# A message-passing network kernel: the first stage's front and second sorting pass are re-ordered, and its scatters may run three block steps further ahead

## The reference

```python
h = jnp.maximum(_layernorm(x, axis=-1), 0.0)
# resmlp(x) = silu(x + silu(silu(x) @ w1 + b1) @ w2 + b2) @ wout
xx = resmlp0(h)
xs, xp, xd = resmlp1(h)[src_j], resmlp2(h)[src_j], resmlp3(h)[src_j]
s = xx + segment_sum(gs * xs, idx_i)
p = segment_sum(gp * xp[:, None, :], idx_i);  d = segment_sum(gd * xd[:, None, :], idx_i)
pa, pb = split(p @ w_pp);  da, db = split(d @ w_pd)
y = s + (pa * pb).sum(-2) + (da * db).sum(-2)
x = x + resmlp4(y)
```

## Time and profile before

| what | us |
|---|---|
| median of 3 runs | 1198.83 (1195.27 to 1198.98) |
| the profiled execution, its own time | 1192.66 |
| its span, from first to last instruction | 1189.2 |
| what lies around the span | 3.46 |
| TensorE busy | 1093.1 (92% of the span), granted clock 0.971 in the mean |
| VectorE, ScalarE, GpSimd busy | 689.1, 738.0, 465.2 |
| first stage: span's start to TensorE's last product of it | about 414 |
| second stage: TensorE's first transposition | 426.83 |

### The profile page before, as it was taken

How to read it: one execution, slowest core, us unless ns; L and a number is a source line. 1 busy time by engine, 2 the same in 40 slices (tenths; PEclk the granted TensorE clock), 3 DMA queues, 4 the chain that set the end, 5 groups by cost and what they waited for, 6 DMA issues and landing times.

```text
span 1189.2 us, 22906 instructions
## 1 busy us (share of the span) xinstructions
PE 1093.1 (92%) x6267; PEld 713.8 (60%) x6267; DVE 689.1 (58%) x2415; ACT 738.0 (62%) x1379; POOL 465.2 (39%) x429
## 2 busy tenths in 40 slices
PE   4878998968999849999999999999979999999998
PEld 2655665745666425666666666666736666666665
DVE  8876876774666316575666556565633444444432
ACT  4657778856777815656655655566536666666664
POOL 2355666034566542665566556555440000000000
PEclk9989999997999959999999999999998999999999
DMA  8667677745664452665655555555549999999984
GB/s 262 201 222 239 216 229 226 286 140 171 199 224 167 162 93 62 120 119 105 103 107 102 104 99 104 101 102 96 103 68 233 277 274 276 271 274 269 269 276 142
DMA packets 319188, 210.81 MB, mean 177 GB/s; under 512 B 204085, under 2 KB 240831, under 8 KB 318964
## 3 DMA queue, kind: packets, MB, share of 16 engines
q1 hardware_dynamic: 280770, 164.67, 50.1%
q0 software_dynamic: 24208, 19.29, 10.2%
q10 hardware_dynamic: 14112, 25.70, 6.1%
HBM read 107.15 MB, written 102.42 MB: 176 GB/s over the span
## 4 chain that ended last, share of the span: by engine, by line
PE 81%; issue 6%; DVE 5%; SPq 2%; ACT 2%; DMA 2%; another core or an unknown queue 1%; POOL 0%; ACTq 0%; POOLq 0%; DVEq 0%
PE quad L1122 7%; PE bank L1136 7%; PE bank L1758 6%; PE quad L871 5%; PE quad L1128 5%; PE bank L1768 5%; PE bank L888 5%; PE bank L1834 4%; PE quad L878 4%; PE bank L1804 4%; PE bank L1835 4%; PE quad L856 2%; PE quad L1111 2%; PE bank L1807 2%; PE quad L1843 2%
## 5 line engine op out<-in xcount | busy, mean ns | idle before, releaser
L1410 POOL DMA_INDIRECT node_sums<-rowout,row_i x98 | 155.4, 1585 | 49.5 <-issue 29.0
L74 POOL DMA_INDIRECT yin<-node_h,er x98 | 99.3, 1014 | 156.6 <-DMA nxt<-edges_by_src 125.0
L1043 DVE TENSOR_TENSOR rowout<-bank,xin 128x512 f32<-128x512 f32 x98 | 67.8, 691 | 142.7 <-PE bank L1136 141.7
L486 POOL DMA_INDIRECT edges_by_src<-pay,rank_i x98 | 97.1, 990 | 103.8 <-DVE rank_i L689 51.3
L888 PEld LDWEIGHTS bank<-wo_sb,s 128*128 128x128 f32 x720 | 95.8, 196 | 60.5 <-issue 60.5
L1136 PEld LDWEIGHTS bank<-wo_sb,s 128*128 128x128 f32 x784 | 102.8, 191 | 47.8 <-issue 47.8
L1462 DVE SCALAR_TENSOR_TENSOR h<-bank,b_sb,hT 128x512 f32<-128x512 f32 (+1 forms) x75 | 55.4, 739 | 125.4 <-PE bank L1768 122.9
L486 POOL DMA_INDIRECT edges_by_low<-pay,rank_i x98 | 97.5, 995 | 68.8 <-issue 27.6
L781 ACT ACTIVATE xn<-xin,nbias,rnorm 128x128 f32<-128x128 f32 x222 | 106.5, 493 | 15.3 <-DVE nbias L604 10.9
L677 DVE SCALAR_TENSOR_TENSOR picked<-bank,onehot 128x256 bf16<-128x256 f32 (+1 forms) x196 | 67.6, 388 | 80.5 <-PE bank L844 59.3
L888 PE MATMUL bank<-wo_sb,s 128*128 128x128 f32 x720 | 98.3, 280 | 10.6 <-issue 7.3
(11 more groups left out here) (210 smaller groups left out, 2279.3 us busy)
## 6 DMA issues: line engine op xcount, KB each, us to landing
xin<-in_x_dram SPq DMA_DIRECT2D x196, 256.0 KB
node_h<-xn SPq DMA_DIRECT2D x98, 256.0 KB
out_dram<-rowout ACTq DMA_DIRECT2D x98, 256.0 KB
node_sums<-rowout SPq DMA_DIRECT2D x90, 256.0 KB
yin<-node_sums SPq DMA_DIRECT2D x53, 256.0 KB, 3.7
yin<-node_sums SPq DMA_DIRECT2D x180, 64.0 KB, 3.2
src_in_every_row<-edge_src_row SPq DMA_DIRECT2D x24, 256.0 KB
border_sums_by_tile<-border_sums SPq DMA_DIRECT2D x24, 256.0 KB, 2.1
```

The lines of the kernel that those rows point to most:

```text
L74: pool.indirect_dma_start(out=xg[:, s, j, :], out_offset=None, in_=x, in_offset=bass.IndirectOffsetOnAxis(ap=er[:, s, j, 1:2].bitcast(mybi ...
L486: nc.gpsimd.indirect_dma_start(out=ps.dram, out_offset=bass.IndirectOffsetOnAxis(ap=rank_i[:, t:t + 1], axis=0), in_=pay[:, t, :], in_offs ...
L1410: nc.gpsimd.indirect_dma_start(out=ysum, out_offset=bass.IndirectOffsetOnAxis(ap=row_i[:, t % 2, j:j + 1], axis=0), in_=urow[:, t % 2, j, ...
```

## The change

1. **Front.** The first batch of statistics that is made into scales is now of two blocks, not four, and the second of six (blocks 2 to 7). The statistics of blocks 2 and 3, and the comparison of digits (`same_digits`), are put between the first batch's norm steps. SyncE issues the stores of h of blocks 0 to 3 between the loads of x of blocks 9 to 19, where all twelve loads stood ahead of them. One group of counts goes from (3, 1) to (4, 0), the seeds stand where they stood, written as a place.
2. **Turn (second pass).** TensorE's counts begin at (49, 1) and end at (52, 1) rather than (53, 0), in groups of growing number. Seeds and bases are at (53, 0) and (53, 1), the picks of chunk 0 at VectorE's step 52 rather than 54, and `chunks` is 53 rather than 54, so that every later chunk comes one step earlier. The comparison of digits is made before the wait for the counts, and the corrections are made by GpSimd, ahead of its scatters. The norm steps of the batch of blocks 56 to 63 (four in each of VectorE's steps 50 to 54 before) stand in steps 53 and 54, ten in each.
3. **Scatters.** `keep_pace` counts from three block steps earlier in both passes: 2 to 42 in the first, 50 to 90 in the second.

```diff
--- before.py
+++ after.py
...
@@ -281,13 +281,13 @@
             m = 0
             BANK_X = (psum[0], psum[1], psum[2], psum[6])
             BANK_A, BANK_COUNT, BANK_RUN, BANK_O = psum[3], psum[4], psum[5], psum[7]
-            places = ((1, 0), (1, 1), (2, 0), (2, 1), (2, 1), (3, 0), (3, 1), (3, 1), (3, 1), (4, 0), (4, 0), (4, 0), (4, 0), (4, 0))
-            again = tuple(p for p in ((50, 0), (50, 1), (51, 0), (51, 1), (52, 0), (52, 1), (53, 0)) for _ in range(2))
-            passes = (Pass(0, {0: (0, 14)}, places, 4, 3, 5, (0, 5), by_low, LOW),
-                      Pass(1, {49: (0, 14)}, again, 53, 54, 54, (49, 54), by_src, HIGH))
+            places = ((1, 0), (1, 1), (2, 0), (2, 1), (2, 1), (3, 0), (3, 1), (3, 1), (4, 0), (4, 0), (4, 0), (4, 0), (4, 0), (4, 0))
+            again = ((49, 1), (50, 0), (50, 1)) + ((51, 0),) * 2 + ((51, 1),) * 2 + ((52, 0),) * 3 + ((52, 1),) * 4
+            passes = (Pass(0, {0: (0, 14)}, places, (4, 1), (5, 0), 3, 5, (0, 5), by_low, LOW),
+                      Pass(1, {49: (0, 14)}, again, (53, 0), (53, 1), 52, 53, (49, 54), by_src, HIGH))
             LN_OPS = 20
             LARGE = 32
-            batches = [(b, 4) for b in range(0, LARGE, 4)] + [(b, min(8, NB - b)) for b in range(LARGE, NB, 8)]
+            batches = [(0, 2), (2, 6)] + [(b, 4) for b in range(8, LARGE, 4)] + [(b, min(8, NB - b)) for b in range(LARGE, NB, 8)]
 
             x_in = [sem(f"n_x_in{i}") for i in range(NX)]
             stored = [sem(f"n_stored{i}") for i in range(4)]
@@ -333,6 +333,8 @@
                         todo = {3: range(1, CH + 1), 4: range(CH + 1, LN_OPS + 1)}
                     else:
                         first, steps = (b - 5, 4) if b <= LARGE else (b - 6, 5)
+                        if any(ps.n and first <= ps.picked_at < first + steps for ps in passes):
+                            first, steps = passes[1].picked_at + 1, 2
                         each = -(-LN_OPS // steps)
                         todo = {first + n: range(1 + each * n, 1 + min(each * (n + 1), LN_OPS)) for n in range(steps)}
                     if B and k in todo:
@@ -429,10 +431,10 @@
                 assert n_rest == N_REST
                 for b in range(8, NX):
                     load_x(b)
-                store_h(0)
-                store_h(1)
+                    if b % 3 == 0:
+                        store_h(b // 3 - 3)
                 for k in range(2, NB + 4):
-                    if k < NB:
+                    if 4 <= k < NB:
                         store_h(k)
                     if k == 6:
                         sp.wait_ge(s_cst, 5)
@@ -472,11 +474,24 @@
                 def keep_pace(ps, t):
 
 
-                    half = 2 * ps.scatters + 5 * t // 6
+                    half = 2 * (ps.scatters - 3) + 5 * t // 6
                     if half % 2 == 0:
                         pool.wait_ge(xT_done, min(half // 2, NK))
                     else:
                         pool.wait_ge(b_done, min(half // 2 - 2, NK))
+
+                def corrections(n):
+
+                    same = equal[:, :, :, :].rearrange("p c j i -> p (c j) i")
+                    pool.wait_ge(s_equal, 4 * n + 1)
+                    nc.gpsimd.tensor_tensor(equal[:, :, :, :], equal[:, :, :, :],
+                                            earlier[:, :, :].unsqueeze(1).to_broadcast([P, CHUNKS, CH, CH]), ALU.mult).then_inc(s_equal, 1)
+                    pool.wait_ge(s_equal, 4 * n + 2)
+                    nc.gpsimd.tensor_tensor(same[:, :, 0:3], same[:, :, 0:3], same[:, :, 3:6], ALU.add).then_inc(s_equal, 1)
+                    pool.wait_ge(s_equal, 4 * n + 3)
+                    nc.gpsimd.tensor_tensor(same[:, :, 0], same[:, :, 0], same[:, :, 1], ALU.add).then_inc(s_equal, 1)
+                    pool.wait_ge(s_equal, 4 * n + 4)
+                    nc.gpsimd.tensor_tensor(corr[:, :], same[:, :, 0], same[:, :, 2], ALU.add).then_inc(s_corr, 1)
 
                 def scatter(ps, c):
                     pool.wait_ge(s_rank, ps.n * CHUNKS + c + 1)
...
@@ -534,6 +540,7 @@
                 for s in s_back:
                     pool.wait_ge(s, 16)
                 pool.wait_ge(s_init, 16 * (-(-SPARE // TB) + len(groups) + ND))
+                corrections(1)
                 for c in range(CHUNKS):
                     scatter(passes[1], c)
                 for s in s_scat:
@@ -642,14 +649,6 @@
                     nc.vector.tensor_copy(digit_f[:, lo:hi], digit_i[:, lo:hi]).then_inc(s_digit, 1)
                     dve.wait_ge(s_digit, steps + 2)
 
-                def corrections(ps):
-
-                    dve.wait_ge(s_equal, 4 + 1)
-                    nc.vector.tensor_tensor(equal[:, :, :, :], equal[:, :, :, :],
-                                            earlier[:, :, :].unsqueeze(1).to_broadcast([P, CHUNKS, CH, CH]), ALU.mult).then_inc(s_equal, 1)
-                    dve.wait_ge(s_equal, 4 + 2)
-                    nc.vector.tensor_reduce(corr[:, :], equal[:, :, :, :].rearrange("p c j i -> p (c j) i"), AX.X, ALU.add).then_inc(s_corr, 1)
-
                 def onehots(ps, k, between):
 
                     for g in range(*ps.made_at[k]):
@@ -704,14 +703,18 @@
                 for b in (0, 1):
                     stats(b, 0, TB)
                 digits(passes[0], 0)
-                same_digits(0)
-                for b in (2, 3):
-                    stats(b, 0, TB)
                 for i in range(1, LN_OPS + 1):
                     norm_step(0, i)
+                    if i == 1:
+                        same_digits(0)
+                    elif i - 2 < 2 * TB:
+                        j = (i - 2) % TB
+                        stats(2 + (i - 2) // TB, j, j + 1)
 
                 for k in range(NB):
                     blocks, todo, pick = stats_at(k), norm_steps_at(k), picks_at(k)
+                    if k == max(passes[1].made_at) + 1:
+                        same_digits(1)
 
                     def next_norm_step():
 
...
@@ -837,6 +837,18 @@
                     nc.tensor.matmul(BANK_COUNT[:, 0:ps.width], ones_h[:, :], counts_h[:, 0:ps.width], start=True, **start).then_inc(s_total, 1)
                     nc.tensor.matmul(BANK_RUN[:, 0:ps.width], before_h[:, :], counts_h[:, 0:ps.width], start=True, **start)
 
+                def bases(ps):
+                    pe.wait_ge(s_base, ps.n + 1)
+                    nc.tensor.matmul(BANK_RUN[:, 0:ps.width], ident[:, :], base[:, 0:ps.width], start=False, **start).then_inc(s_run, 1)
+
+                def seeds_or_bases(place):
+
+                    for ps in passes:
+                        if place == ps.seeded_at:
+                            seeds(ps)
+                        if place == ps.based_at:
+                            bases(ps)
+
                 def running(ps, c):
 
                     pe.wait_ge(s_pick, (ps.n * CHUNKS + c) * CH)
@@ -856,11 +868,9 @@
                             last = nc.tensor.matmul(BANK_X[k % 4][:, j * P:(j + 1) * P], xn[:, k % 4, j, :], ident[:, :],
                                                     start=j == 0, stop=False, is_transpose=True, skip_group_check=True)
                         last.then_inc(xT_done, 1)
+                    seeds_or_bases((k, 0))
                     for ps in passes:
-                        if k == ps.chunks:
-                            pe.wait_ge(s_base, ps.n + 1)
-                            nc.tensor.matmul(BANK_RUN[:, 0:ps.width], ident[:, :], base[:, 0:ps.width], start=False, **start).then_inc(s_run, 1)
-                        elif ps.chunk(k):
+                        if ps.chunk(k):
                             running(ps, ps.chunk(k))
                     if 0 <= k - 1 < NK:
                         pe.wait_ge(s1_done, k)
@@ -877,9 +887,7 @@
                         pe.wait_ge(s2_done, k - 1)
                         nc.tensor.matmul(BANK_X[(k - 2) % 4][:, :], w2_sb[:, m, :], s2[:, (k - 2) % 3, :], start=False, stop=True,
                                          skip_group_check=True).then_inc(b_done, 1)
-                    for ps in passes:
-                        if k == ps.seeded_at:
-                            seeds(ps)
+                    seeds_or_bases((k, 1))
                     if 0 <= k - 3 < NA:
                         pe.wait_ge(s3_done, k - 2)
                         if k >= 4:
```

18 lines of the change are left out of this document (3 added, 15 removed).

## The result

The changed kernel takes 1251.08 us (median of 4, 1241.48 to 1255.96) against 1197.05 of the kernel before in the same session: ratio 1.0425, 95% interval 1.0386 to 1.0464. The forecast was 1191.9 us. The profiled execution took 1247.28 us, 54.6 more than the one before. Nearly all of it is lost in the first stage, as VectorE's first transposition of the sorted edges in the second stage shows. First the kernel before, then the changed one; the columns are start, duration, engine, line and operation.

What follows compares the result with a forecast made beforehand. TensorE bounds the kernel; time is to be had only in the first stage, where it idles at the front, the turn and beside scatters. 3.3 + 3.6 + 0 = 6.9 us off 1198.83 gives 1191.9 us, range 1184 to 1201.

Steps and rivals of the forecast that it cites:

- Part 3: Scatters of both passes let go three block steps earlier: 0 us, bounds 3.1 us gained and 15 lost.
- Rival (c): Chunks 3 to 10 of each pass: back-to-back scatters make it slower, 1207.3 us at 0.1 us per scatter; chance 0.13.
- its deciding point of 0.045 us: Price per scatter, 6.9 us over 154 scatters, from which unpaced scatters would decide the outcome.
- (c)'s mechanism: Dense scatters hold up landings of stores of h and node_sums; with four-tile rings ScalarE stops, then TensorE.
- Part 1, the front: Start of the first stage, to 51 us: counts copied at 36.7 instead of 39.99; gain 3.3 us, bounds 2.1 and 3.3.
- VectorE's 1.2 us: At the front, pairing statistics with norm steps takes VectorE 4.6 us against 5.8, so 1.2 us less.
- the scale for block 2: At the front, it comes 1 us after ScalarE could use it; taken as 0, since TensorE waits for one-hots behind it.
- Rival (b): Front or turn: one gain is swallowed by late loads, a late store or a poor turn; 1194.7 to 1198 us; chance 0.22.
- Part 2, the turn: Turn to the second sorting pass, 241 to 259 us: block 56 sooner; gain 3.6 us, bounds 0.8 and 4.9.
- The clock term: Behind the shorter idle before block 56, TensorE's clock stays at 1.00 instead of 0.50: 1.5 us, bounds 0 and 1.5.

Runs made afterwards that it cites:

- e5: The changed kernel run again, on a chip where the kernel before takes about 1199 us: 1260.64 us, ratio 1.0487.
- e10: The changed kernel, its scatters three steps earlier, with GpSimd clearing a scratch tile of 384 columns after each scatter: 1167.28 us, ratio 0.9802.
- e7: The kernel before with only the front changed, old scatter pace, on a stalling chip: ratio 1.0015.
- e2: The kernel before with only the scatters' pace three block steps earlier, on a quiet chip (kernel before 1120.7 us): ratio 0.9998.
- e3: The kernel before with only the scatters' pace one block step earlier, on a quiet chip: ratio 0.9993.
- e4: The kernel before with only the scatters' pace one block step later, on a quiet chip: ratio 1.0008.
- e1: The changed kernel with the scatters' old pace, front and turn still changed, on a quiet chip: ratio 0.9971.
- e6: The kernel before, unchanged, run for a trace of its own on a stalling chip: 1199.45 us.
- e8: The kernel before with only the turn changed, old scatter pace, on a stalling chip: ratio 0.9938.
- e9: The kernel before with only the scatters' pace three block steps earlier, on a stalling chip: 1260.25 us, ratio 1.0578.

## Why the prediction was wrong, by its own steps

**Part 3 is the step that failed.** I took 0 for the lead, with a bound of 15 us lost (0.1 us for each of 154 scatters). Measured alone it is 67.9 us, 0.44 us each, over four times the bound. Rival (c) had the right sign and place, and its deciding point of 0.045 us each was passed tenfold; I gave it 0.13. Three things misled me. First, I priced the unpaced scatter from the mean of paced ones (0.21 us of idle each); but that mean covers runs of different length. Split by length of run in the trace of before, each run with the pause behind it, TensorE idles 16.5 of 167.5 us (10%) with runs of up to four scatters, 15.3 of 121.5 (13%) with runs of five to seven, and 9.9 of 27.5 (36%) with the two longer ones, of 8 and 11: 0.52 us for each of their 19 scatters. So sign and size both stood there, on few scatters. "Nothing here shows a paced and an unpaced run of the same chunk" was true only to the letter, for paced and unpaced runs of different chunks are there: the second pass of the kernel before opens with eleven scatters without a pause (253.2 to 266.9), and in the midst of them TensorE stands still up to

```profile
267.78 1.09 PE L856 MATMUL quad<-ident,xn 128*128 128x128 f32 x4 [5.62 <-issue]
```

Second, "GpSimd is busy for 96.6 of 160 us, so even unpaced chunks leave gaps": the gaps lie between the runs, not in them, and a dense run of a whole chunk or two is what the lead makes. Third, I argued that the number and bytes of the transfers don't change ("the total of stores and scatters is the same"); they are the same in e5 and e10, and 6.9% (1.0487 against 0.9802), some 82 us, lie between them.

My reading of why the old pace helps, argued and not tested: it ties the scatters to TensorE's steps, so that a stall, which holds up TensorE, also holds up the next scatters; with the lead they go on.

Of (c)'s mechanism only half stands. What comes late is the word of TensorE's products and of VectorE's steps, not the landing of a store (the waits for landings above), and the rings of four tiles are not where it begins. The Trainium skill, "DMA: Bandwidth & Descriptors", section "Queues, rings and completion order", which I had set against the change, speaks of increments of DMAs; it pointed the right way, but the late release in the stall above is of no DMA, and no run here tests that rule.

**Part 1, the front: nothing or a small loss instead of 3.3.** e7 gives 1.0015 (0.9988 to 1.0042). The traces are sharper than the times. Ten traces with the old order at the front have block 7 at 49.86 to 50.99 us (median 50.25), ten with the new order at 51.09 to 51.44 (median 51.23): about 1.0 us later. The copy of the counts stands at 38.36 to 39.99 in the old order, at 40.08 to 40.43 in the new; the trace from which I took 39.99 and 50.99 has the latest of both. The first store of h did land in time, as forecast: ScalarE's waiting for it is gone. Two terms failed. One is VectorE's 1.2 us. In the changed kernel (VectorE, then GpSimd):

```profile
7.12 0.28 DVE L560 BATCH_NORM_STATS2 stat<-xin 128x6 f32<-128x128 f32 x1
7.32 1.30 DVE L584 TENSOR_TENSOR lnt<-lnt 128x8 f32<-128x8 f32 x1
8.54 0.28 DVE L560 BATCH_NORM_STATS2 stat<-xin 128x6 f32<-128x128 f32 x1
8.75 0.70 DVE L586 TENSOR_SCALAR means<-lnt 128x8 f32<-128x8 f32 x1
7.00 1.60 POOL L487 TENSOR_TENSOR equal<-equal,earlier 128x686 f32<-128x686 f32 x1 [1.64 <-DVE equal L367]
8.68 0.74 POOL L490 TENSOR_TENSOR equal<-equal 128x294 f32<-128x294 f32 x1
```

A step of 0.17 us takes 1.30 and ends when GpSimd's operation ends (8.62 and 8.60), the next 0.70; the statistics between them keep their 0.28. Before, statistics alone stood beside GpSimd's first operation, and one step of 0.72 us beside its second; I had priced a pair of statistic and step by 0.29 us from a place where GpSimd did nothing. The Trainium skill, "GPSIMD Engine Reference", section "1. Specifications", says that GpSimd shares SBUF interfaces with VectorE and gets in its way when a VectorE instruction has two SBUF inputs; the step of 1.30 us is one with two such inputs, and agrees. The first batch's last step (nbias) starts at 13.08 instead of 12.16: 0.9 us later, not 1.2 earlier.

The other is the scale for block 2, which now comes out of the second batch. I had put that at 0, because TensorE would wait for one-hots behind it. But ScalarE waits for it 2.02 us, TensorE has block 2 at 24.42 instead of 22.18, and from there to 40.3 it is never idle, so that nothing of this comes back (ScalarE, then TensorE):

```profile
22.15 1.26 ACT L781 ACTIVATE xn<-xin,nbias,rnorm 128x128 f32<-128x128 f32 x3 [2.02 <-DVE nbias L611]
24.42 0.66 PE L868 MATMUL quad<-ident,xn 128*128 128x128 f32 x4 [1.47 <-ACT xn L781]
```

The counts were copied and block 7 came at

```profile
40.43 0.42 DVE L746 CAST counts_h<-bank 128x256 bf16<-128x256 f32 x1 [1.47 <-PE bank L831]
```
```profile
51.44 0.66 PE L868 MATMUL bank<-ident,xn 128*128 128x128 f32 x4 [2.35 <-issue]
```

instead of the forecast 36.7 and 47.7. Rival (b) had "the front brings nothing", for another reason.

**Part 2, the turn: right, and at its upper bound.** It reads best on the quiet chip, where scatters disturb nothing. From TensorE's transposition of block 50 to that of block 60 it takes 46.37, 46.39 and 46.40 us in e2, e3 and e4, and 41.43 in e1: 4.95 us less, where I had 3.6, bounds 0.8 and 4.9. The idle time ahead of block 56 went from 3.47 to 0.55 us (forecast 1.4), first e2, then e1:

```profile
224.89 0.83 PE L856 MATMUL quad<-ident,xn 128*128 128x128 f32 x4 [3.47 <-DVE xn L623]
226.00:228.00 2.00, 2.00 (x8) 1.33 (x6) 1.37 (x8) 0.73 (x2) 1.51 (x2) 0.50 0.99 306
```
```profile
221.41 0.66 PE L868 MATMUL quad<-ident,xn 128*128 128x128 f32 x4 [0.55 <-DVE xn L630]
222.00:224.00 2.00, 2.00 (x9) 1.04 (x8) 2.00 (x11) 2.00 (x5) 1.70 (x2) 1.00 0.78 273
```

The clock term came too: the granted clock was 0.50 behind the long idle time, 1.00 behind the short one. It is not the same in every execution, though: in e6 the clock was 1.00 in 258 to 262, behind 3.48 us of idle time. With a front 1.0 us slower, 4.95 - 1.0 makes 4.0 us, which is what lies between the medians there (1120.7 and 1116.7; by the ratio 3.2, interval 2.2 to 4.4).

On the stalling chip e8 gives 0.9938, 8.1 us between the medians (4.3 to 10.6 by its interval). The idle time ahead of block 56 fell from 3.48 (e6) to 1.50 us (e8):

```profile
258.21 0.66 PE L856 MATMUL quad<-ident,xn 128*128 128x128 f32 x4 [3.48 <-DVE xn L623]
```
```profile
253.75 0.63 PE L866 MATMUL quad<-ident,xn 128*128 128x128 f32 x4 [1.50 <-issue]
```

From block 50 to block 60 it is 54.08 us in e6 and 47.69 in e8; e6 has a stall of 5.12 us ahead of block 58 that e8 has not. The second pass now begins a step sooner, which also moves its scatters, and I had missed that. That this gives the rest was not tested.

**The sum.** Over one session each, the three parts were 0, 8 and -68 us (e7, e8, e9), together 60 us slower, where 3.3 + 3.6 + 0 had been forecast faster; 54 and 61 were measured. Of the signs that I had named, (c)'s (25 us or more of idle time in each scatter stretch: 48.0 and 35.3) came. (b)'s (copy at 38 us or later) came as well but was no sign, since it holds for the kernel before too.
